# Second layer norm and router logits computed block by block inside the attention, with the kept rows added back in the expert loop

## The reference, cut to what matters

```python
h = _layernorm(x, ln1_g, ln1_b)
q, k, v = h @ wq + bq, h @ wk + bk, h @ wv + bv      # 8 heads of 32
attn = softmax(q @ k.T / sqrt(32))                   # over all tokens
x = x + (attn @ v) @ wo + bo
h2 = _layernorm(x, ln2_g, ln2_b)                     # the second norm
probs = softmax(h2 @ router_w + router_b)            # the logits
# top 2 of 8 experts, a capacity of 666 tokens each, the last expert to pick a token wins
moe_out[t] = gelu(h2[t] @ w1[e] + b1[e]) @ w2[e] + b2[e]
return x + moe_out
```

## Time and profile before

| | us |
|---|---|
| median of 3 runs | 2833.61 (2833.28 to 2833.88) |
| the profiled execution, whole | 2833.08 |
| its span in the trace | 2831.3 |
| PE busy | 2478.9 (88%) |
| DVE busy | 2026.2 (72%) |
| ACT busy | 1576.9 (56%) |
| POOL busy | 1283.3 (45%) |

### The profile page before, as it was taken

How to read it: one execution, slowest core, us unless ns; L and a number is a source line. 1 busy time by engine, 2 the same in 40 slices (tenths; PEclk the granted TensorE clock), 3 DMA queues, 4 the chain that set the end, 5 groups by cost and what they waited for, 6 DMA issues and landing times. The chain is left out here.

```text
span 2831.3 us, 54629 instructions
## 1 busy us (share of the span) xinstructions
PE 2478.9 (88%) x20934; PEld 1926.4 (68%) x20934; DVE 2026.2 (72%) x3022; ACT 1576.9 (56%) x2658; POOL 1283.3 (45%) x749
## 2 busy tenths in 40 slices
PE   4879929999969998759999999999999999248995
PEld 3668819999968887735666666666666665148995
DVE  5775558888868866647777877777777774447885
ACT  4554417777744543315666666666666666226773
POOL 0001002222224302335888888888888888402331
PEclk9999959999989999968999999999999999658997
DMA  9986326666747754352000000220000000115664
GB/s 398 361 327 228 94 86 217 234 234 233 227 162 233 236 171 129 102 132 70 11 15 16 9 17 14 45 55 11 15 16 9 16 14 2 61 68 210 232 233 169
DMA packets 110400, 361.81 MB, mean 128 GB/s; under 512 B 21888, under 2 KB 48896, under 8 KB 92416
## 3 DMA queue, kind: packets, MB, share of 16 engines
q1 hardware_dynamic: 89152, 295.43, 30.4%
q0 software_dynamic: 18464, 55.59, 6.3%
q10 hardware_dynamic: 2592, 8.16, 0.7%
HBM read 314.30 MB, written 44.83 MB: 127 GB/s over the span
## 5 line engine op out<-in xcount | busy, mean ns | idle before, releaser
L1347 POOL TENSOR_TENSOR at_pool_sum<-at_pool_sum,at_probs 128x1024 f32<-128x1024 f32 x364 | 865.9, 2379 | 100.8 <-ACT at_probs L1473 60.2
L1502 DVE TENSOR_REDUCE at_part_max<-ps_x 128x2 f32<-128x1024 f32 x624 | 734.4, 1221 | 228.5 <-PE ps_x L1403 228.5
L1473 ACT ACTIVATE at_probs<-ps_s 128x512 f32<-128x512 f32 x1352 | 698.2, 604 | 325.3 <-PE ps_s L1362 301.2
L1362 PE MATMUL ps_s<-at_qst,at_kst 97*128 97x256 f32 x2704 | 518.4, 312 | 4.8 <-ACT at_probs L1473 4.0
L1362 PEld LDWEIGHTS ps_s<-at_qst,at_kst 97*128 97x128 f32 x2704 | 369.7, 190 | 217.7 <-ACT at_probs L1473 123.6
L1379 PE MATMUL ps_oz<-at_probs,k_xhat 128*32 128x256 f32 (+1 forms) x5408 | 392.4, 387 | 0.0
L577 PE MATMUL ps_acc<-adj_hi,y_hi 128*128 128x512 f32 (+1 forms) x728 | 289.8, 398 | 91.9 <-DVE adj_lo L643 61.5
L643 DVE TENSOR_TENSOR adj_lo<-adj_raw,adj_hi 128x1024 fp32r<-128x1024 f32 (+1 forms) x182 | 217.6, 1197 | 164.9 <-ACT adj_hi L419 162.7
L579 PE MATMUL ps_acc<-adj_hi,y_lo 128*128 128x512 f32 (+1 forms) x728 | 278.4, 382 | 0.0
L578 PE MATMUL ps_acc<-adj_lo,y_hi 128*128 128x512 f32 (+1 forms) x728 | 278.4, 382 | 0.0
L1011 ACT ACTIVATE ex_hid<-ps_ex_h,ex_b 128x256 f32<-128x256 f32 x432 | 197.2, 475 | 127.7 <-PE ps_ex_h L955 114.7
(11 more groups left out here) (220 smaller groups left out, 4020.9 us busy)
## 6 DMA issues: line engine op xcount, KB each, us to landing
ex_w<-w SPq DMA_DIRECT2D x108, 1024.0 KB, 7.6
adj_raw<-adjT SPq DMA_DIRECT2D x156, 512.0 KB, 4.8
k_xhat<-adj SPq DMA_DIRECT2D x26, 1664.0 KB, 7.9
at_qst<-qk_parts SPq DMA_DIRECT2D x78, 128.0 KB, 2.7
results<-ex_res POOLq DMA_DIRECT2D x34, 256.0 KB, 3.3
ex_b<-b SPq DMA_DIRECT2D x54, 128.0 KB, 2.3
adj_raw<-adjT_tail SPq DMA_DIRECT2D x26, 256.0 KB, 2.7
qk_parts<-qk_hi POOLq DMA_DIRECT2D x26, 256.0 KB, 2.8
```

The lines of the kernel that those rows point to most:

```text
L1347: pool.tensor_tensor(pool_sum[:, g % 2], pool_sum[:, g % 2], probs[:, tile % RING], ALU.add).then_inc(pool_added, 1)
L1362: last = pe.matmul(ps_s[:, unit % S_BANKS, hh, :], kst[:, 2 * j + hh, k * P:(k + 1) * P], qst[:, g % 2, 2 * j + hh, :], start=True, stop=True)
L1473: act.activation(probs[:, tile % RING, 2 * j:2 * j + 2], ps_s[:, unit % S_BANKS], ACT.Exp, scale=scale).then_inc(taken, 1)
L1502: dve.tensor_reduce(part_max[:, g % 2, heads, qt, kc], ps_x[:, pair, :], AX.X, ALU.max).then_inc(x_free, 1)
```

## The change

1. In `attend`, for each block g of the second half of the heads, the second norm of its two tiles is made two blocks later by DVE, in steps spread over cycles 0 to 9 (`norm`): the statistics, then the inverse root by an integer guess and three Newton steps on [128, 2] or [128, 1] operands, then the normed rows into a tile `normal`. The constants are read from a small SBUF tile `numbers` that POOL fills at the start. SP stores the two tiles to `moe_rows` (`store_rows`).
2. Two new job kinds follow, "turn" in cycle 11 (four transposes on PE; DVE copies them out of PSUM with ln2_g and ln2_b applied) and "logits" in cycle 12 (four products with the router; DVE copies them to `m.logits`). Two blocks' worth of cycles are added at the end, for blocks 24 and 25.
3. `second_mixture`, `normalise`, `gate_logits` and `transposed_products` are gone.
4. In the expert loop of layer 1 the gathered rows are not yet scaled: ACT applies ln2_g and ln2_b as it takes them out of PSUM, in two Identity activations, and then makes `rt_hi` from that tile by a third.
5. `x_kept` is loaded by one transfer on ACT's queue into `m.xhat` once the row list is found, and POOL adds it to `m.x` in 7 parts, one after each of the stores of chunks 2 to 8.
6. ln2_g and ln2_b move from broadcast rows to columns.

```diff
@@ attention_jobs
-    for cycle in range(-MAX_AHEAD, BLOCKS * CYCLES + OUT_AT + 1):
+    for cycle in range(-MAX_AHEAD, (BLOCKS + 1) * CYCLES + LOGITS_AT + 1):
...
+        if c == TURN_AT and g >= NCH + 2:
+            now.append(("turn", g - 2, 0, 0, 0))
+        if c == LOGITS_AT and g >= NCH + 2:
+            now.append(("logits", g - 2, 0, 0, 0))
@@ attend, SP
+            def store_rows(g):
+                b = g % NCH * CHUNK
+                sp.wait_ge(normed, 2 * (g - NCH) + 2)
+                sp.dma_start(m.rows_d[b:b + CHUNK, :].rearrange("(k p) d -> p k d", p=P), normal[:]).then_inc(rows_kept, 16)
...
+                if g >= NCH + 4:
+                    store_rows(g - 4)
+            for g in range(BLOCKS - 4, BLOCKS):
+                store_rows(g)
+            sp.wait_ge(rows_kept, 16 * NCH)
@@ attend, POOL
+            for n, value in enumerate((LN_EPS, -0.5, 1.5, ROOT_GUESS)):
+                pool.memset(numbers[:, n:n + 1], value).then_inc(numbered, 1)
+                pool.wait_ge(numbered, n + 1)
@@ attend, PE
+                elif kind == "turn":
+                    pe.wait_ge(normed, 2 * (g - NCH) + 2)
+                    for i in range(QT):
+                        for j in range(KT):
+                            last = pe.transpose(ps_x[:, pair, i * D + j * P:i * D + (j + 1) * P], normal[:, i, j * P:(j + 1) * P], m.ident[:])
+                elif kind == "logits":
+                    pe.wait_ge(x_free, turn_job[g] + 1)
+                    for i in range(QT):
+                        for j in range(KT):
+                            last = pe.matmul(ps_x[:, pair, i * EXPERTS:(i + 1) * EXPERTS], xt[:, i, j, :], m.router[:, j, :],
+                                             start=j == 0, stop=j == KT - 1)
@@ attend, DVE
+                elif kind == "turn":
+                    both = ps_x[:, u % 2 * 2, :].rearrange("p (i j n) -> p i j n", i=QT, j=KT)
+                    for j in range(KT):
+                        last = dve.tensor_scalar(xt[:, :, j, :], both[:, :, j, :], m.cols[:, 8 + j:9 + j], m.cols[:, 10 + j:11 + j], ALU.mult, ALU.add)
+                    last.then_inc(x_free, 1)
+                elif kind == "logits":
+                    b = g % NCH * QT
+                    dve.tensor_copy(m.logits[:, b:b + QT, :].rearrange("p t e -> p (t e)"), ps_x[:, u % 2 * 2, 0:QT * EXPERTS]).then_inc(x_free, 1)
...
+            def norm(g, c):
+                b = g % NCH * QT
+                tiles = range(QT)
+                if c == 0:
+                    dve.wait_ge(numbered, 4)
+                    dve.wait_ge(x_free, out_job[g] + 1)
+                    for i in tiles:
+                        steps.inc(dve.bn_stats(st[:, i, :], m.x[:, b + i, :]))
+                elif c == 1:
+                    steps.settle(dve)
+                    for i in tiles:
+                        steps.inc(dve.bn_aggr(mv[:, i, :], st[:, i, :]))
+                    steps.settle(dve)
+                    steps.inc(dve.tensor_scalar(var[:], mv[:, :, 1], numbers[:, 0:1], None, ALU.add))
+                elif 2 <= c <= 7:
+                    steps.settle(dve)
+                    if c == 2:
+                        steps.inc(dve.tensor_scalar(root[:].bitcast(I32), var[:].bitcast(I32), numbers[:, 1:2], numbers[:, 3:4], ALU.mult, ALU.add))
+                        steps.settle(dve)
+                    if c % 2 == 0:
+                        for i in tiles:
+                            steps.inc(dve.tensor_scalar(bend[:, i:i + 1], root[:, i:i + 1], root[:, i:i + 1], var[:, i:i + 1], ALU.mult, ALU.mult))
+                    else:
+                        steps.inc(dve.tensor_scalar(bend[:], bend[:], numbers[:, 1:2], numbers[:, 2:3], ALU.mult, ALU.add))
+                        steps.settle(dve)
+                        for i in tiles:
+                            steps.inc(dve.tensor_scalar(root[:, i:i + 1], root[:, i:i + 1], bend[:, i:i + 1], None, ALU.mult))
+                elif c in (8, 9):
+                    i = c - 8
+                    steps.settle(dve)
+                    if g > NCH:
+                        dve.wait_ge(rows_kept, 16 * (g - NCH))
+                    dve.tensor_scalar(normal[:, i, :], m.x[:, b + i, :], mv[:, i, 0:1], root[:, i:i + 1], ALU.subtract, ALU.mult).then_inc(normed, 1)
...
                 for job in jobs[cycle]:
                     take(job)
+                if g >= NCH + 2:
+                    norm(g - 2, c)
@@ expert_layers, ACT
-                act.activation(rt_hi[:], ps_t[:, :, 0:CHUNK], ACT.Copy).then_inc(rows_hi, 1)
+                if second:
+                    for j in range(KT):
+                        act.activation(rt[:, j, :], ps_t[:, j, 0:CHUNK], ACT.Identity, bias=m.cols[:, 10 + j:11 + j],
+                                       scale=m.cols[:, 8 + j:9 + j]).then_inc(rows_even, 1)
+                    act.wait_ge(rows_even, n * 2 + 2)
+                    act.activation(rt_hi[:], rt[:], ACT.Copy).then_inc(rows_hi, 1)
...
+            if second:
+                act.wait_ge(found, 1)
+                act.dma_start(m.xhat[:].rearrange("p t d -> p (t d)"), m.x_kept).then_inc(x_back, 16)
             prepare(0, 0)
@@ expert_layers, POOL
+            def add_back(c):
+                at = slice(first_tile(c), first_tile(c + 1))
+                pool.wait_ge(x_back, 16)
+                pool.tensor_tensor(m.x[:, at, :], m.x[:, at, :], m.xhat[:, at, :], ALU.add).then_inc(back_added, 1)
...
                 store(n)
+                if second and 2 <= n < 2 + CHUNKS:
+                    add_back(n - 2)
```

More of the change, by code:

```diff
@@ L108, in inverse_root @@
         c.settle(dve)
[L111 to L201, removed]
@@ L676, in lift_product @@
                 dve.wait_ge(produced, k + 1)
-                dve.tensor_tensor(m.xhat[:, k, :], ps_v[:, 0:D], m.rows[:, 4, :], ALU.add)
+                dve.tensor_tensor(m.xhat[:, k, :], ps_v[:, 0:D], m.rows[:, 2, :], ALU.add)
                 if k >= 2:
@@ L879, in expert_layers @@
     found, listed = s("ex_found"), s("ex_listed")
+    second = layer == 1
+    rows_even, x_back, back_added = s("ex_rows_even"), s("ex_x_back"), s("ex_back_added")
     stored, res_free = [s("ex_stored0"), s("ex_stored1")], s("ex_res_free")
@@ L894, in expert_layers @@
         rows = sb("rows", [P, 2, TT, D])
+        rt = sb("rt", [P, KT, CHUNK]) if second else None
         rt_hi, rt_lo = sb("rt_hi", [P, KT, CHUNK], F32R), sb("rt_lo", [P, KT, CHUNK], F32R)
@@ L1025, in prepare @@
                 dve.wait_ge(rows_hi, n + 1)
[L1026 removed]
+                dve.tensor_tensor(rt_lo[:], rt[:] if second else ps_t[:, :, 0:CHUNK], rt_hi[:].bitcast(F32), ALU.subtract).then_inc(rows_lo, 1)
                 for layer in range(2):
@@ L1165, in _ @@
             act.wait_ge(put, 16 * CHUNKS)
-def gate_logits(nc, m, s, src, w, rows):
-    def products(pe, xt, ps):
-        for j in range(KT):
-            last = pe.matmul(ps[:, 0, 0:EXPERTS], xt[:, j, :], w[:, j, :], start=j == 0, stop=j == KT - 1)
-        return last
-    def take_act(act, k, ps, took):
-        act.activation(m.logits[:, k, :], ps[:, 0, 0:EXPERTS], ACT.Copy).then_inc(took, 1)
-    def take_dve(dve, k, ps, act_took, took):
-        dve.sem_inc(took, 1)
-    transposed_products(nc, m, s, src, products, take_act, take_dve, 1, rows)
 def mixture(nc, m, t, s, layer, bias, capacity, chunks, results, out, idle_pool=None):
@@ L1246, in attend @@
     out_job = {job[2]: job[0] for job in flat if job[1] == "out"}
+    turn_job = {job[2]: job[0] for job in flat if job[1] == "turn"}
     last_max = {job[2]: job[0] for job in flat if job[1] == "tail"}
@@ L1393, in run @@
                     pe.wait_ge(x_free, u - 1)
-                if g == 0 and kind != "out" and qt == hp == 0:
+                if g == 0 and kind in ("max", "tail") and qt == hp == 0:
                     pe.wait_ge(first_keys[kc], 16)
@@ L1442, in _ @@
                 for job in jobs[cycle]:
-                    if job[1] != "out":
+                    if job[1] in ("max", "tail"):
                         run(job)
@@ L1455, in _ @@
                 for job in jobs[cycle]:
-                    if job[1] == "out":
+                    if job[1] not in ("max", "tail"):
                         run(job)
@@ L1523, in _ @@
             dve.wait_ge(x_free, len(flat))
-def second_mixture(nc, m, t, s, out):
-    normalise(nc, m, s, m.x, m.xhat)
-    scaled, loaded, added = s("ln2_scaled"), s("x_back"), s("back_added")
-    with nc.sbuf_tensor(named("x_back"), [P, NT, D], F32) as back, nc.Block() as block:
-        @block.sync
-        def _(sp):
-            sp.dma_start(back[:].rearrange("p t d -> p (t d)"), m.x_kept).then_inc(loaded, 16)
-        @block.gpsimd
-        def _(pool):
-            pool.wait_ge(loaded, 16)
-            pool.tensor_tensor(m.x[:], m.x[:], back[:], ALU.add).then_inc(added, 1)
-            pool.wait_ge(added, 1)
-        @block.vector
-        def _(dve):
```

(6 more changed lines are left out.)

33 lines of the change are left out of this document (23 added, 10 removed).

## The result

| | before | after |
|---|---|---|
| median, us | 2833.45 (2832.47 to 2833.88, 4 runs) | 2873.11 (2866.07 to 2873.28, 4 runs) |
| profiled execution / its span, us | 2833.08 / 2831.3 | 2866.07 / 2864.3 |

The account below looks back on a forecast made before the run. PE was taken to bound the attention and the experts, a chain the stage between. From 2833.08 us, 67.0 - 17.6 - 0.95 - 6.3 - 3 = 39.2 less gave a forecast of 2794, range 2778 to 2816.

Parts of the forecast that it names:

- The step that failed: Attention, DVE: the norm's small operations don't wait for POOL's adds, so no time is added for that.
- The prediction's own sign of being wrong: Small DVE operations of over 0.5 us, PE's max products waiting for DVE, Identity table loads, or chunks as short as before.
- Rival 1: Attention, DVE: 19 small operations a block wait about half a POOL add, 176 us more in all, 2970; chance 0.06.
- PE's turn and logits: Inside the attention, on PE: 1.6 us for each of eleven blocks, 17.6 us in all.
- DVE's norm fits a cycle: Attention, cycles 1 to 9: DVE's work with the norm is 3.10 us a cycle against 3.12, so cost 0.
- The end of the attention: Last add to routing: the old stage goes and a shorter tail comes, so routing starts 67.0 us earlier.
- the 3.0 of block 24: End of the attention: block 24's norm between the last reciprocals and the last add takes 3.0 us.
- block 25's norm: End of the attention, in the open: statistics, 19 small operations and two applies take 4.4 us together.
- the scale and shift: Experts, ACT: 0.95 us more on the first chunk, then 0.33 on each of 19 later chunks, 6.3 us.
- The load of the kept rows: Start of the experts: sharing with the first gathers and second chunk's weights costs 3 us, bounds 0 and 11.
- POOL's adds: Experts: seven adds of 2.7 us each lie in POOL's idle time, two chunks ahead of a need.
- table load: Experts, ACT: forecast none; a rival had one per Identity and Gelu, 26 us more, 2820, chance 0.03.

Follow-up runs that it names:

- e9_forms: The kernel before with 36 more DVE tensor_scalar in the norm: 256, 512 and 1024 elements, none, one or two per-partition operands; 2892.39 us beside 2871.59.
- e4_pad1: The kernel before with four idle one-element DVE tensor_scalar in each of blocks 15 to 25; 2875.62 us beside 2874.86.
- e1_unit: The changed kernel with the norm's two-element operations each written as two one-element ones; 2877.45 us, ratio 1.001 to the kernel before.
- e2_unit_act: e1_unit with the norm's two applies made by ACT, DVE making only a one-element shift; 2845.10 us, ratio 0.9901 to the kernel before.
- e7_kept: e2_unit_act with the kept x loaded by SP and added by POOL inside the attention, not in the experts; 2804.34 us, kernel before 2835.59.
- e8_both: e7_kept with ACT writing rt_hi straight from PSUM and DVE making the exact rt beside it; 2792.79 us, ratio 0.9851 to the kernel before.
- e6_noadd: e2_unit_act without POOL's seven adds of the kept x in the experts, their load staying; 2804.14 us, kernel before 2835.59.

## Why the prediction was wrong

**The step that failed** is the one on whether the small operations wait for POOL: "the form with per-partition operands moves one element at a time, half the cast's pace ... By the row these instructions aren't in that mode, and the sum stays". One row gives one point, not a pace. 407 ns for 256 elements against 427 for 512 looked like half the speed; by e9_forms it is 161 ns fixed, 133 for the elements at the cast's pace and 59 for each of two operands, 412 for the 407. The prediction's own sign of being wrong, small operations of over 0.5 us on DVE and max products waiting for DVE, is what came. The Trainium skill's rule (SBUF — State Buffer, "Who interferes with whom"), which the prediction set aside, held: `tensor_scalar` can use the pair of ports shared with GpSimd, and whoever comes second is blocked fully; the ends at 2210.18 and 2224.61 show it in the attention. The rows of the experts differ: there the operation that is on record first, by 0.22 to 0.53 us, was the one held, so the profile's starts don't tell who comes second. The Trainium skill (VectorE: DVE Perf Modes, "Mode 2×_2P — use both read ports for one tensor") asks for one source, both tensors in SBUF, and an outermost dimension, not counting dimensions of one, that is even, or odd and equal in both; the runs agree for [128,2], waiting up to 2441 ns. Of [128,1], which has no such dimension, the section says nothing; it never took over 267 in e4_pad1.

**Rival 1 was the mechanism, with a chance of 0.06 and too large a price.** It let all 19 operations wait, 16 us a block. Only two-element ones (three a block) and an apply do, and a block lost about 50.8 - 45.1 = 5.7. Of the 78.0 us that the attention grew from first to last block, the turn and the logits are 17.0, the two-element operations 32.9 and the applies 28.1, by e1_unit and e2_unit_act. A second reading of the same growth: from the 15th copy of `at_oz` to the last (1945.32 to 2496.86; before 1947.56 to 2421.05) PE stood idle 551.54 - 518.96 = 32.6 us against 4.5, and the clock gave away 22.2 (half of the time that it was granted at 0.50), against none. With the 17.0 of the turn and the logits that is 67.3 of the 78.0; the other 10.7 are not assigned. So over a quarter of the growth is PE running at its lower level, and the rival, which priced waits alone, had no such term; its total was still too large, since 16 of its 19 operations in a block don't wait (twelve of one element, the two aggregates, the guess and one L1499 that falls between adds).

**PE's turn and logits**: right, 1.58 a block for 1.6, and 17.0 for 17.6.

**DVE's norm fits a cycle**: right for the work itself (45.08 a block in e2_unit_act, though with the applies on ACT), wrong for the waits, which the prediction put at nothing.

**The end of the attention**: nearly right, 20.08 for 17.2 (with the 3.0 of block 24 counted in both). Part of the 2.9 missed is block 25's norm: 2506.62 to 2512.55, 5.9 for 4.4, although POOL is idle by then.

```profile
2506.62 0.74 DVE L1483 BATCH_NORM_STATS2 at_st<-k_x 128x6 f32<-128x256 f32 x2
...
2508.27 0.46 DVE L1497 TENSOR_SCALAR at_bend<-at_root,at_var 128x1 f32<-128x1 f32 x2
2508.76 0.29 DVE L1499 TENSOR_SCALAR at_bend<-at_bend,at_numbers 128x2 f32<-128x2 f32 x1
...
2511.82 0.73 DVE L1508 TENSOR_SCALAR at_normal<-k_x,at_mv,at_root 128x256 f32<-128x256 f32 x2
...
2517.57 0.37 DVE L678 TENSOR_TENSOR rt_mask<-k_logits,k_bias 128x208 f32<-128x208 f32 x1 [0.55 <-PEq L1183]
```

The middle of a Newton step (L1499) is 0.29 and a pair 0.46, with a gap of 0.03 between, where 0.15 to 0.195 an operation was taken from two-tensor operations without such operands: that fits the 59 ns per operand, but was not tried at this size.

**The experts**: the scale and shift were sized too small. They delay `w_hi` by 1.08 us (1.58 for 0.50), near the 0.95, but a chunk grew by about 0.6 and not by 0.33: the 0.62 us between `w_lo` and PE was only in part slack (a hand-over is in it; this is argued, the 0.6 a chunk is measured). In all 13.4 for 7.3, by e7_kept and e8_both, so with the adds away. The load of the kept rows was 4.1 for 3. POOL's adds, at zero because POOL is idle, cost 4.1: the idle engine was POOL, the one that waited was DVE, which has two-tensor subtractions from SBUF all through a chunk (3.47 for 0.69, and never over 0.77 without the adds in e6_noadd). No table load came with the Identity: ACT's line of the Gelu has 25 loads as before, and L903 none.

## What to carry to other kernels

Where POOL is busy with adds in SBUF, a DVE operation is to be priced by its form and not by its size: in these kernels `tensor_scalar` of one element per partition never waited, of two or more (float32, from SBUF to SBUF) it waited to the end of the running add, and a cast of 512 elements and subtractions of two SBUF tensors were held for a whole add. Before it is concluded from one row that an operation runs at a slow pace, the fixed part has to be taken off with a second size. And PE's short waits for another engine can cost nearly as much again in granted clock (22.2 us beside 28.1 more of idle time here).

## What was not expected of the hardware

- A per-partition operand costs about 59 ns per instruction at 256, 512 and 1024 elements alike (294, 353 and 413 ns for 256 with none, one, two; 694 and 814 for 1024 with none and two).
- A `tensor_scalar` on [128,2] took up to 2.44 us beside a POOL add of 2.4, on [128,1] at most 0.27. Reciprocals, 337 to 355 ns in the changed kernel, did not wait, though 64 of them start while an add runs.
- After PE's waits of 0.65 and 0.62 us at 2226.36 and 2227.49 its granted clock was 0.50 (1.2 of 2.4 GHz) from about 2229 to 2243, though PE was busy all of that time. The like pair at 2211.95 and 2213.07 was not followed by such a fall, so what decides is not told by these rows. From 1950 to 2498 the clock fell nine times, each time right behind such a pair, and PE's longest gap in that stretch was 0.91 us.
- What stays open: why three of four executions of the changed kernel took 7 us longer than the profiled one (where a DVE operation falls against an add would do it, and this was only argued), and how much of e8_both's gain would remain on the chips with longer chunks, where it was not run.
